# Loading the stacks of a transformer block's queries and keys in halves of 8 heads, into 48, 32 and 16 partitions at a time

## The chip, the cores and the metric

The kernel runs on one core of a Trainium2 chip. The metric is the device time of one execution in microseconds; lower is better.

## The reference

One block of a conditioned transformer over a batch of 8 sequences of 512 tokens with 256 features, in 16 heads of 16, all in float32:

```python
c6 = silu(c) @ Wc + bc                                    # shift, scale, gate, twice
xm = ln(x) * (1 + sc_msa) + sh_msa
q = (xm @ Wq + bq).reshape(B, S, 16, 16) / 16             # k, v likewise, not divided
w = softmax(einsum('bqhc,bkhc->bhqk', q, k))
y = einsum('bhqk,bkhc->bqhc', w, v).reshape(B, S, 256)
x = x + g_msa * (y @ Wo + bo)
xm2 = ln(x) * (1 + sc_mlp) + sh_mlp
x = x + g_mlp * (gelu(xm2 @ W1 + b1) @ W2 + b2)           # W1: 256 x 1024
```

## The kernel before

All work is done for one batch element after another in a software pipeline written out by hand. Pass i does four things side by side: it projects batch i+2 to queries, keys and values (`has_a`), computes the plain scores of batch i+1 and takes their row maxima (`scores`, `row_max`, 64 blocks of 128 x 512), computes the transposed scores, the exponentials and the product with the values of batch i, and the MLP of batch i-1. Passes run from -2 to 8; passes 2 to 5 are a loop of two bodies, the others are written out. A pass with all parts first goes through 16 attention steps, then the projections, then the MLP, and ends with the projection of the attention's output (`wo_products`), in whose middle `first_transposed` computes the first transposed scores of the next pass. Each engine has its own program, and semaphores tie them.

**Stacks.** The scores need float32 accuracy, and run in bf16. So each query and each key is split in three bf16 parts (high, middle, low), and the six products of parts that count are summed by one matmul over 96 partitions: six slots of 16 partitions, each the 16 features of a head, in `qst` the parts `QPARTS`, in `kst` the parts `KPARTS`. The free axis holds 16 heads x 512 tokens. The projections leave features on partitions (`j` = 0, 1 for the two halves of the queries, 2, 3 of the keys), so that the heads have to be moved: ScalarE, VectorE and GpSimd form the three parts of a j in `parts` (semaphores `part_h`, `part_m`, `part_l`), `write_parts` on SyncE writes them to DRAM (384 KB for each j), and `load_stack` reads them back, one DMA for each slot, six for the queries and six for the keys of a batch. `parts_written[w]` counts the writes of the queries and of the keys, `stack_loaded` all twelve loads. There are two pairs of stacks, used in turn.

**Maxima.** When the 64 maxima of a batch are there, TensorE turns them (`turn_maxima`), VectorE splits them in two bf16 rows (`maxima_rows`, `mrow_done`), and SyncE loads them into two more partitions of `qst`, opposite rows of -1 in `kst` (`load_maxima`, `m_loaded`; for the first half of batch 0's heads `half_loaded`). So the transposed scores come out with the maximum taken off. `first_transposed` waits for it.

**Order on SyncE's queue in a pass.** Outputs of the attention (`y_scr`), writes of j = 0 and 1, reciprocal sums to `r_scr` (after `rec_done`), writes of j = 2 and 3, `rb` (the reciprocals, broadcast, which VectorE needs for `y_norm(0)`), loads of the query stack, loads of the key stack, maxima, output of the batch before, next input. All DMAs are issued by SyncE. In the prologue, batch 1's parts are written only when batch 0's stacks are loaded, and its stacks are loaded only when GpSimd has read the weights staged in them (`const_set`, 6).

Of the kernel before, what the change touches and what calls it, by code (L numbers as in the profile page):

```python
# [25 lines left out]
ALU = mybir.AluOpType  # L26
# [3 lines left out]
NB, S, H = 8, 512, 256  # L30
# [3 lines left out]
KC = H // P  # L34
TT = S // P
JT = MLP // P
QPARTS = (0, 0, 1, 1, 0, 2)
KPARTS = (0, 1, 0, 1, 2, 0)
NSLOT = len(QPARTS)
MROW = NSLOT * DH  # L40
KROWS = MROW + 2
G = 4
# [23 lines left out]
def dit_block(nc, x, c, Wc, bc, Wq, bq, Wk, bk, Wv, bv, Wo, bo, W1, b1, W2, b2, out,  # L66
              c6_scr, parts_scr, y_scr, r_scr):
    with ExitStack() as ctx:
# [85 lines left out]
        rest_done = sem("rest_done")  # L154
        part_m = sem("part_m")
        part_l = sem("part_l")
        parts_written = [sem(f"parts_written_{n}") for n in "qk"]
        stack_loaded = sem("stack_loaded")
        v_done = sem("v_done")
        vaug_done = sem("vaug_done")  # L160
        s_done = sem("s_done")
# [87 lines left out]
        def _(sp):  # L249
# [24 lines left out]
            def step(i, par):  # L274
                if runs(i, 2) and later(i, 2, 1) and not early(i) or early(i) and not later(i, 2, 1):
                    b = i + 3 if early(i) else i + 2
                    sp.wait_ge(tp_done[0], b)
                    sp.dma_start(xa[:], x[bass.ds(b, 1)].rearrange("o (t p) f -> p (o t) f", p=P)).then_inc(xa_loaded, 16)
                if runs(i, 0):
                    if later(i, 0, 1):  # L280
                        sp.wait_ge(x1_done, i)
                    sp.dma_start(xd[:], x[bass.ds(i, 1)].rearrange("o (t p) f -> p (o t) f", p=P)).then_inc(xd_loaded, 16)
                    sp.dma_start(ga[:], c6_scr[bass.ds(i, 1), G1 * H:(G1 + 1) * H].broadcast_to([P, H])).then_inc(ga_loaded, 16)
                if runs(i, -1):
                    if later(i, -1, 1):
                        sp.wait_ge(o_gated, i - 1)
                    sp.dma_start(gm[:], c6_scr[bass.ds(i - 1, 1), G2 * H:(G2 + 1) * H].broadcast_to([P, H])).then_inc(gm_loaded, 16)

                def load_maxima(stack, first, last, loaded):

                    for n in range(2):
                        sp.dma_start(stack[MROW + n:MROW + n + 1, first:last, :], mrow[0:last - first, n, :]).then_inc(loaded, 16)

                if runs(i, 0) and not later(i, 0, 1):
                    sp.wait_ge(mrow_done, 2)
                    load_maxima(qst[par], NH // 2, NH, m_loaded)
                if runs(i, 0):


                    for g in range(NG):  # L300
                        sp.wait_ge(y_evac, NG * i + g + 1)
                        sp.dma_start(y_scr[G * g:G * (g + 1)].rearrange("h r s -> (h r) s"), ysb[:, g % 2, :]).then_inc(y_written[g % 2], 16)
                    for n in range(2):
                        sp.wait_ge(y_written[n], 32 * i + 32)
                    sp.dma_start(den, y_scr[:, DH, :].rearrange("h (a s) -> h a s", s=NH * S // P)).then_inc(den_loaded, 16)
                    sp.wait_ge(xg_done, i + 1)
                    for k in range(KC):
                        sp.dma_start(yc[:, k, :], y_scr[8 * k:8 * k + 8, 0:DH, :]).then_inc(yc_loaded, 16)

                def write_parts(b, j):  # L310
                    sp.wait_ge(part_l, 4 * b + j + 1)
                    m = j % 2
                    sp.dma_start(parts_scr[j // 2, :, m * P:(m + 1) * P, :].rearrange("n p s -> p n s"),
                                 parts[:, j, :, :]).then_inc(parts_written[j // 2], 16)

                def load_stack(b, w):


                    sp.wait_ge(parts_written[w], 32 * b + 32)
                    for slot in range(NSLOT):  # L320
                        stk, which = (qst, QPARTS) if w == 0 else (kst, KPARTS)
                        sp.dma_start(stk[par][slot * DH:(slot + 1) * DH, :, :],  # L322
                                     parts_scr[w, which[slot]].rearrange("(h d) s -> d h s", d=DH)).then_inc(stack_loaded, 16)

                if early(i) and later(i, 2, 1):
                    sp.wait_ge(stack_loaded, 192)
                if runs(i, 2):
                    write_parts(i + 2, 0)
                    write_parts(i + 2, 1)
                if runs(i, 0):  # L330
                    sp.wait_ge(rec_done, i + 1)
                    sp.dma_start(r_scr.rearrange("h (a s) -> (h a) s", s=NH * S // P), rec).then_inc(r_written, 16)
                if runs(i, 2):
                    write_parts(i + 2, 2)
                    write_parts(i + 2, 3)
                if runs(i, 0):
                    sp.wait_ge(r_written, 16 * i + 16)
                    for k in range(KC):
                        sp.dma_start(rb[:, k, :], r_scr[8 * k:8 * k + 8].unsqueeze(1).broadcast_to([8, DH, S])).then_inc(rb_loaded, 16)
                if runs(i, 2):  # L340
                    if early(i) and later(i, 2, 1):

                        sp.wait_ge(c6_written, 16)
                        sp.wait_ge(prep_pe, 4)
                        sp.wait_ge(w_split, 2)
                    load_stack(i + 2, 0)
                    if early(i) and later(i, 2, 1):
                        sp.wait_ge(const_set, 6)
                    load_stack(i + 2, 1)
                if early(i) and runs(i, 1):  # L350
                    sp.wait_ge(half_rows, 2)
                    load_maxima(qst[1 - par], 0, NH // 2, half_loaded)
                elif runs(i, 1):
                    sp.wait_ge(mrow_done, 2 * i + 4)
                    load_maxima(qst[1 - par], 0, NH, m_loaded)
                if runs(i, -1):
                    sp.wait_ge(o_done, i)
                    sp.dma_start(out[bass.ds(i - 1, 1)].rearrange("o (t p) f -> p (o t) f", p=P), osb[:]).then_inc(out_written, 16)
# [5 lines left out]
        def _(pool):  # L364
# [31 lines left out]
            def step(i, par):  # L396
# [32 lines left out]
                if runs(i, 2):  # L429
                    b = i + 2  # L430
                    for j in range(4):
                        if j == 2 and runs(i, -1):
                            z_lo(1, i - 1)
                        pool.wait_ge(part_m, 4 * b + j + 1)
                        pool.tensor_tensor(parts[:, j, 2, :], rest[:, j % 2, :], parts[:, j, 1, :], ALU.subtract).then_inc(part_l, 1)  # L435
                    if early(i) and later(i, 2, 1):
                        mlp_weights()
                if runs(i, -1):
# [12 lines left out]
        def _(act):  # L451
# [33 lines left out]

            def step(i, par):
                if runs(i, 0):
                    for w in range(2):
                        act.wait_ge(parts_written[w], 32 * (i + 2) if runs(i, 1) else 32 * NB)
                    for s in range(STEPS):  # L490
                        for p in range(2):
                            act.wait_ge(st_done, 32 * i + 2 * s + p + 1)
# [16 lines left out]
                if runs(i, 2):  # L509
                    b = i + 2  # L510
                    for j in range(4):
                        act.wait_ge(qk_done, 4 * b + j + 1)
                        if j % 2 == 0 and later(i, 2, 1) and not runs(i, 0):
                            act.wait_ge(parts_written[j // 2], 32 * b)
                        act.activation(parts[:, j, 0, :], ps[:, QK_BANKS[j], :], ACT.Identity,
                                       bias=bqk[:, j // 2, j % 2:j % 2 + 1]).then_inc(part_h, 1)
                    for n in range(2):
                        act.wait_ge(v_done, 2 * b + n + 1)
                        act.activation(vaug[par][:, 2 * n:2 * n + 2, :, 0:DH],
                                       ps[:, 4 + n, :].rearrange("p (t h d) -> p t h d", t=2, d=DH), ACT.Copy).then_inc(vaug_done, 1)  # L520
# [24 lines left out]
        def _(pe):  # L545
# [36 lines left out]
            def scores(i, par, blocks, banks=(6, 7)):  # L582

                for _ in range(blocks if runs(i, 1) else 0):
# [2 lines left out]
                    h, t = n // TT, n % TT  # L587
                    if n >= len(banks):
                        pe.wait_ge(max_done, 64 * (i + 1) + n - len(banks) + 1)
                    elif n == 0:  # L590
                        pe.wait_ge(stack_loaded, 192 * (i + 2))
                        if later(i, 1, 1):
                            pe.wait_ge(mrow_done, 2 * (i + 1))
                    pe.matmul(ps[:, banks[n % len(banks)], :], qst[1 - par][0:MROW, h, t * P:(t + 1) * P], kst[1 - par][0:MROW, h, :],  # L594
# [211 lines left out]
        def _(dve):  # L806
# [115 lines left out]
            def step(i, par):  # L922
# [36 lines left out]
                def rest_of(b, j):  # L959
# [4 lines left out]
                    elif early(i) and later(i, 2, 1):  # L964
                        dve.wait_ge(part_l, 4 * b + j - 1)
                    dve.scalar_tensor_tensor(out=rest[:, j % 2, :], in0=ps[:, QK_BANKS[j], :], scalar=bqk[:, j // 2, j % 2:j % 2 + 1],
                                             in1=parts[:, j, 0, :], op0=ALU.add, op1=ALU.subtract).then_inc(rest_done, 1)
                    dve.wait_ge(rest_done, 4 * b + j + 1)
                    dve.tensor_copy(parts[:, j, 1, :], rest[:, j % 2, :]).then_inc(part_m, 1)  # L969

# [98 lines left out]
_INS = ["x", "cond_1024"] + ["L0_cond_" + n for n in ("Wc", "bc", "Wq", "bq", "Wk", "bk", "Wv", "bv", "Wo", "bo", "W1", "b1", "W2", "b2")]  # L1069


# [21 lines left out]
```

## Time and profile before

| | us |
|---|---|
| median of 3 runs | 865.38 |
| lowest, highest | 861.15, 870.09 |
| profiled execution, first to last instruction (its own time is not given beside it) | 857.3 |
| TensorE, VectorE, ScalarE, GpSimd busy in it | 725.0, 582.5, 384.3, 222.2 |
| TensorE's mean granted clock | 0.906 |
| moved by DMA | 75.87 MB in 68,774 packets |

The profile is of one execution. Times in its rows are microseconds from the first instruction. In a timeline, a row gives the start, the length, the engine (SPq is SyncE's queue of DMA issues, whose length is that of issuing and not of moving), the line, the operation, what it writes and reads, how many are merged, and in brackets the idle time before it with what ended it. Neighbouring matmuls overlap, so merged lengths are rough. L594 are the plain scores, L624 the transposed ones, L732 and L724 the output projection, L895 the row maxima, L313 the writes of parts, L322 the loads of the stacks, L292 the loads of the maxima.

### The profile page before, as it was taken

How to read it: one execution, taken by the hardware profiler on the slowest of the kernel's cores; microseconds unless marked ns; L12 is line 12 of the kernel's file. 1: busy time of each engine (PE TensorE's matmuls, PEld its weight loads, DVE VectorE, ACT ScalarE, POOL GpSimd, SP SyncE). 2: the span in 40 equal slices, each digit the busy share in tenths (PEclk: the TensorE clock that was granted, in tenths of full speed). 3: DMA queues.
4: the chain of work that ended last, by engine and by line, in shares of the span. 5: the costliest groups of instructions: out<-in, count | busy, mean ns of one | idle time of the engine just before them, and what ended most of it. 6: DMA issues, size and time to landing. Idle time of an engine off the chain costs nothing.

```text
span 857.3 us, 11761 instructions
## 1 busy us (share of the span) xinstructions
PE 725.0 (85%) x3967; PEld 390.6 (46%) x3967; DVE 582.5 (68%) x1015; ACT 384.3 (45%) x462; POOL 222.2 (26%) x163
## 2 busy tenths in 40 slices
PE   4648589865999599995999599997999798999987
PEld 1531122422247432682257522682258422851776
DVE  5728588863987488874987388875987587560373
ACT  0410156303763177423763167424762376269321
POOL 4262001200316103430315103430325030331244
PEclk9775599956999899997999799998999899899998
DMA  7499700295018910395028910393028611111210
GB/s 262 121 122 161 117 14 26 95 160 94 25 52 152 143 53 25 125 136 113 26 70 143 138 52 25 129 145 100 26 88 148 107 45 36 43 63 37 65 31 24
DMA packets 68774, 75.87 MB, mean 88 GB/s; under 512 B 6214, under 2 KB 59996, under 8 KB 68716
## 3 DMA queue, kind: packets, MB, share of 16 engines
q1 hardware_dynamic: 68716, 75.10, 43.5%
q8 instruction: 35, 0.57, 0.3%
q14 instruction: 23, 0.19, 0.1%
HBM read 49.35 MB, written 25.48 MB: 87 GB/s over the span
## 4 chain that ended last, share of the span: by engine, by line
issue 36%; PE 30%; DVE 11%; POOL 10%; DMA 7%; SPq 3%; ACT 2%; POOLq 0%; DVEq 0%; ACTq 0%
PE ps L616 6%; PE ps L594 6%; PE ps L624 5%; DVE mx L895 5%; PE ps L549 4%; POOL hl L442 4%; PE ps L755 3%; DMA qst<-mrow 3%; SPq L322 3%; DMA kst<-parts_scratch 2%; POOL prob L435 2%; PE ps L759 2%; ACT prob L497 1%; POOL x L415 1%; POOL xd L428 1%
## 5 line engine op out<-in xcount | busy, mean ns | idle before, releaser
L895 DVE TENSOR_REDUCE mx<-ps 128x1 f32<-128x512 f32 x512 | 335.9, 686 | 83.8 <-PE ps L594 80.0
L497 ACT ACTIVATE prob<-ps 128x1024 f32<-128x1024 f32 x256 | 247.9, 1022 | 237.4 <-PE ps L624 237.0
L594 PE MATMUL ps<-kst,qst 96*128 96x512 bf16 x512 | 201.5, 417 | 33.9 <-DVE mx L895 17.5
L624 PE MATMUL ps<-qst,kst 98*128 98x512 bf16 x512 | 156.9, 402 | 60.6 <-DMA qst<-mrow 52.9
L594 PEld LDWEIGHTS ps<-kst,qst 96*128 96x128 bf16 x512 | 46.1, 99 | 204.0 <-DVE mx L895 166.7
L616 PE MATMUL ps<-prob,vaug 128*32 128x512 f32 x1024 | 137.3, 608 | 0.4 <-ACT prob L497 0.3
L442 POOL TENSOR_TENSOR hl<-z,hh 128x512 fp32r<-128x512 f32 x64 | 82.3, 1286 | 138.6 <-DVE hh L1024 138.6
L624 PEld LDWEIGHTS ps<-qst,kst 98*128 98x128 bf16 x512 | 48.8, 102 | 130.1 <-DMA qst<-mrow 54.2
L536 ACT ACTIVATE z<-ps,bias_t 128x512 f32<-128x512 f32 x64 | 44.0, 688 | 135.7 <-PE ps L759 130.1
L390 POOL TENSOR_TENSOR rstd<-vare,mhalf 128x4 f32<-128x4 f32 x16 | 16.3, 1021 | 330.4 <-DVE vare L835 330.4
L549 PE MATMUL ps<-w_hi,hh 128*128 128x256 f32 x256 | 73.6, 287 | 0.3 <-POOL hl L442 0.3
L435 POOL TENSOR_TENSOR prob<-prob 128x512 bf16<-128x512 f32 x32 | 37.3, 1167 | 140.3 <-DVE prob L969 140.3
L549 PE MATMUL ps<-w_hi,hl 128*128 128x256 f32 x256 | 72.0, 281 | 0.0
L549 PE MATMUL ps<-w_lo,hh 128*128 128x256 f32 x256 | 71.9, 281 | 0.0
L755 PE MATMUL ps<-zh,w_hi 128*128 128x512 f32 x128 | 61.1, 478 | 2.0 <-DVE zh L900 2.0
L1024 DVE CAST hh<-z 128x512 fp32r<-128x512 f32 x64 | 37.0, 579 | 35.3 <-ACT z L536 35.3
L1010 DVE TENSOR_TENSOR x<-ps,ga 128x1024 f32<-128x1024 f32 x7 | 8.6, 1225 | 75.3 <-PE ps L732 75.3
L755 PE MATMUL ps<-zh,w_lo 128*128 128x512 f32 x128 | 51.9, 405 | 0.0
L549 PEld LDWEIGHTS ps<-w_hi,hh 128*128 128x128 f32 x256 | 48.2, 188 | 2.9 <-POOL hl L442 0.8
L549 PEld LDWEIGHTS ps<-w_lo,hh 128*128 128x128 f32 x256 | 48.2, 188 | 1.8
L549 PEld LDWEIGHTS ps<-w_hi,hl 128*128 128x128 f32 x256 | 48.2, 188 | 0.0
L759 PE MATMUL ps<-zl,w_hi 128*128 128x512 f32 x128 | 41.7, 407 | 0.1
(106 smaller groups left out, 858.6 us busy)
## 6 DMA issues: line engine op xcount, KB each, us to landing
parts_scratch<-prob SPq DMA_DIRECT2D x32, 384.0 KB, 2.6
qst<-parts_scratch SPq DMA_DIRECT2D x48, 256.0 KB, 11.2
kst<-parts_scratch SPq DMA_DIRECT2D x48, 256.0 KB, 17.6
y_scratch<-rb SPq DMA_DIRECT2D x32, 256.0 KB, 2.0
xa<-in_x_dram SPq DMA_DIRECT2D x8, 512.0 KB, 9.4
xd<-in_x_dram SPq DMA_DIRECT2D x8, 512.0 KB, 3.5
yc<-y_scratch SPq DMA_DIRECT2D x16, 256.0 KB
rb<-r_scratch SPq DMA_DIRECT2D x16, 256.0 KB
```

What stands on the lines that cost most here:

```text
L435: pool.tensor_tensor(parts[:, j, 2, :], rest[:, j % 2, :], parts[:, j, 1, :], ALU.subtract).then_inc(part_l, 1)
L442: pool.tensor_tensor(hl[:, j % HR, :], hb[:, j % HB, :], hh[:, j % HR, :].bitcast(F32), ALU.subtract).then_inc(hl_done, 1)
L497: act.activation(prob[:, s % 2, 2 * p:2 * p + 2, :], ps[:, 2 * p:2 * p + 2, :], ACT.Exp, scale=1.0 / DH).then_inc(exp_done, 1)
L536: act.activation(hb[:, j % HB, :], ps[:, 4 + j % 2, :], ACT.Gelu, bias=b1_t[:, j:j + 1]).then_inc(gelu_done, 1)
L549: m = pe.matmul(out_, a, b, start=start and n == 0, stop=stop and n == 2, skip_group_check=True)
L594: pe.matmul(ps[:, banks[n % len(banks)], :], qst[1 - par][0:MROW, h, t * P:(t + 1) * P], kst[1 - par][0:MROW, h, :], start=True, stop=True ...
L616: m = pe.matmul(ps[32 * q:32 * q + 32, 4 + g % 2, :], vaug[par][:, kt, G * g + q, :], prob[:, s % 2, q, :], start=kt == 0, stop=kt == TT - ...
L624: m = pe.matmul(ps[:, q, :], kst[par][0:KROWS, G * g + q, kt * P:(kt + 1) * P], qst[par][0:KROWS, G * g + q, :], start=True, stop=True)
L755: pe.matmul(ps[:, 4 + j % 2, :], w1[n][:, k, f], zh_of(1, b)[:, k, :], start=k == 0 and n == 0, stop=False)
L759: m = pe.matmul(ps[:, 4 + j % 2, :], w1[0][:, k, f], zl_of(1, b)[:, k, :], start=False, stop=k == KC - 1)
L895: dve.tensor_reduce(mx[:, t, h:h + 1], ps[:, banks[n % len(banks)], :], AXX, ALU.max).then_inc(max_done, 1)
L1024: dve.tensor_copy(hh[:, j % HR, :], hb[:, j % HB, :]).then_inc(hh_done, 1)
```

## The change

- Within each j, the features are ordered by their place in the head first and by the head second, through permuted columns of Wq, bq, Wk and bk, laid out where the arrays are handed to the kernel. `parts_scr` becomes `(4, 3, 128, 512)`, one block for each j, in which the 8 heads of one feature lie together.
- The parts are stored in such an order (`PART_AT`) that slots 0 to 2 hold parts 0 to 2, slots 3 and 4 two neighbouring parts, slot 5 one. So three DMAs load a half: into 48, 32 and 16 partitions, 8 heads each (`SLOT_RUNS`).
- `load_stack(b, w, m)` loads half m of the queries (w = 0) or keys. Each j has its own semaphore of writes, each half of the heads its own of loads, and the scores of heads 0 to 7 wait for the first halves alone.
- On SyncE's queue each query half is issued ahead of the write of a keys' part; `rb` comes between those writes and the loads of the keys' halves. The prologue's waits move along.
- ScalarE waits for the four writes one by one.

```diff
-QPARTS = (0, 0, 1, 1, 0, 2)
-KPARTS = (0, 1, 0, 1, 2, 0)
-NSLOT = len(QPARTS)
+NSLOT = 6
+PART_AT = ((0, 1, 2), (2, 1, 0))
+SLOT_RUNS = (((0, 0, 3), (3, 0, 2), (5, 0, 1)), ((0, 0, 3), (3, 1, 2), (5, 2, 1)))
...
                 def write_parts(b, j):
                     sp.wait_ge(part_l, 4 * b + j + 1)
-                    m = j % 2
-                    sp.dma_start(parts_scr[j // 2, :, m * P:(m + 1) * P, :].rearrange("n p s -> p n s"),
-                                 parts[:, j, :, :]).then_inc(parts_written[j // 2], 16)
-
-                def load_stack(b, w):
-
-
-                    sp.wait_ge(parts_written[w], 32 * b + 32)
-                    for slot in range(NSLOT):
-                        stk, which = (qst, QPARTS) if w == 0 else (kst, KPARTS)
-                        sp.dma_start(stk[par][slot * DH:(slot + 1) * DH, :, :],
-                                     parts_scr[w, which[slot]].rearrange("(h d) s -> d h s", d=DH)).then_inc(stack_loaded, 16)
+                    sp.dma_start(parts_scr[j].rearrange("n p s -> p n s"), parts[:, j, :, :]).then_inc(parts_written[j], 16)
+
+                def load_stack(b, w, m):
+
+                    stk = (qst, kst)[w][par]
+                    sp.wait_ge(parts_written[2 * w + m], 16 * b + 16)
+                    for slot, part, n in SLOT_RUNS[w]:
+                        sp.dma_start(stk[slot * DH:(slot + n) * DH, 8 * m:8 * m + 8, :],
+                                     parts_scr[2 * w + m, part:part + n].rearrange("n (d h) s -> (n d) h s", d=DH))\
+                            .then_inc(stack_loaded[m], 16)
 
                 if early(i) and later(i, 2, 1):
-                    sp.wait_ge(stack_loaded, 192)
+                    for m in range(KC):
+                        sp.wait_ge(stack_loaded[m], 96)
...
                 if runs(i, 2):
+                    if early(i) and later(i, 2, 1):
+
+                        sp.wait_ge(c6_written, 16)
+                        sp.wait_ge(prep_pe, 4)
+                        sp.wait_ge(w_split, 2)
+                    load_stack(i + 2, 0, 0)
                     write_parts(i + 2, 2)
+                    load_stack(i + 2, 0, 1)
                     write_parts(i + 2, 3)
...
                 if runs(i, 2):
                     if early(i) and later(i, 2, 1):
-
-                        sp.wait_ge(c6_written, 16)
-                        sp.wait_ge(prep_pe, 4)
-                        sp.wait_ge(w_split, 2)
-                    load_stack(i + 2, 0)
-                    if early(i) and later(i, 2, 1):
                         sp.wait_ge(const_set, 6)
-                    load_stack(i + 2, 1)
+                    load_stack(i + 2, 1, 0)
+                    load_stack(i + 2, 1, 1)
...
-                    elif n == 0:
-                        pe.wait_ge(stack_loaded, 192 * (i + 2))
+                    if t == 0 and h % 8 == 0:
+                        pe.wait_ge(stack_loaded[h // 8], 96 * (i + 2))
+                    if n == 0:
...
+QK_FEATURES = tuple("L0_cond_" + n for n in ("Wq", "bq", "Wk", "bk"))
...
+        if name in QK_FEATURES:
+            a = a.reshape(a.shape[:-1] + (KC, NH // KC, DH)).swapaxes(-1, -2).reshape(a.shape)
...
-    args.append(nc.dram_tensor("parts_scratch", (2, 3, H, S), _mybir.dt.bfloat16).ap())
+    args.append(nc.dram_tensor("parts_scratch", (2 * KC, 3, P, S), _mybir.dt.bfloat16).ap())
```

## Rows read from the trace of the kernel before

**Rows 1.** The page: busy shares, and the DMA line of the 40 slices.

```profile
PE 725.0 (85%) x3967; PEld 390.6 (46%) x3967; DVE 582.5 (68%) x1015; ACT 384.3 (45%) x462; POOL 222.2 (26%) x163
...
DMA  7499700295018910395028910393028611111210
```

**Rows 2.** The list of waits: who waited for whom; us in total, times, longest us.

```profile
PE ps L624 <- DMA qst<-mrow: 52.9, 6, 12.5
...
PE ps L594 <- DMA kst<-parts_scratch: 13.7, 1, 13.7
```

**Rows 3.** Timeline of TensorE around the loads of the maxima: start us, us, line, tiles, idle.

```profile
202.62 1.89 PE L624 MATMUL ps<-qst,kst 98*128 98x512 bf16 x4 [12.50 <-DMA qst<-mrow]
...
490.01 1.89 PE L624 MATMUL ps<-qst,kst 98*128 98x512 bf16 x4 [9.07 <-DMA qst<-mrow]
...
758.55 1.04 PE L624 MATMUL ps<-qst,kst 98*128 98x512 bf16 x4
```

**Rows 4.** Timeline of SyncE's queue of DMA issues in three passes: start us, us, how many.

```profile
168.74 0.33 SPq L332 DMA_DIRECT2D r_scratch<-rb  x1
...
454.82 0.33 SPq L332 DMA_DIRECT2D r_scratch<-rb  x1
...
456.30 1.22 SPq L339 DMA_DIRECT2D rb<-r_scratch  x2
...
460.69 10.69 SPq L322 DMA_DIRECT2D kst<-parts_scratch  x6
477.66 1.20 SPq L292 DMA_DIRECT2D qst<-mrow  x2
...
755.42 1.20 SPq L292 DMA_DIRECT2D qst<-mrow  x2
```

**Rows 5.** Windows: length and each engine's busy us, TensorE's granted clock, DMA share, GB/s.

```profile
72.00:98.00 26.00, 18.18 (x34) 3.41 (x33) 20.68 (x35) 0.00 (x0) 0.00 (x0) 0.50 1.13 121
...
484.00:490.00 6.00, 0.00 (x0) 0.00 (x0) 0.00 (x0) 0.00 (x0) 0.00 (x0) 0.53 1.03 181
68.00:72.00 4.00, 4.00 (x9) 0.68 (x7) 4.00 (x8) 0.00 (x0) 2.23 (x1) 0.50 1.09 380
3.00:8.00 5.00, 0.00 (x0) 0.00 (x0) 3.60 (x1) 1.36 (x2) 5.00 (x1) 1.00 1.01 381
```

**Rows 6.** Timelines of the prologue: SyncE's queue, TensorE, GpSimd, ScalarE.

```profile
32.91 5.15 SPq L313 DMA_DIRECT2D parts_scratch<-prob  x4
...
88.96 1.47 SPq L292 DMA_DIRECT2D qst<-mrow  x2
...
66.56 19.34 PE L594 MATMUL ps<-kst,qst 96*128 96x512 bf16 x34 [13.65 <-DMA kst<-parts_scratch]
...
98.84 1.44 PE L624 MATMUL ps<-qst,kst 98*128 98x512 bf16 x3 [6.65 <-issue]
...
58.76 4.49 POOL L382 TENSOR_TENSOR w_lo<-kst,w_hi 128x2048 fp32r<-128x2048 f32 x1
...
49.65 1.26 ACT L515 ACTIVATE prob<-ps,bias_t 128x512 bf16<-128x512 f32 x2 [1.88 <-PE ps L701]
```

**Rows 7.** The page's DMA issues: how many, KB each, median us from issue to landing.

```profile
parts_scratch<-prob SPq DMA_DIRECT2D x32, 384.0 KB, 2.6
...
kst<-parts_scratch SPq DMA_DIRECT2D x48, 256.0 KB, 17.6
...
vaug<-in_L_cond_Wc_dram SPq DMA_DIRECT2D x1, 768.0 KB, 4.4
```

**Rows 8.** Timeline of VectorE in two passes.

```profile
470.71 1.22 DVE L990 TENSOR_TENSOR yc<-yc,rb 128x1024 f32<-128x1024 f32 x1
...
479.08 1.22 DVE L1048 TENSOR_TENSOR xn<-ps,gm 128x1024 f32<-128x1024 f32 x1
...
493.64 1.23 DVE L1010 TENSOR_TENSOR x<-ps,ga 128x1024 f32<-128x1024 f32 x1 [12.08 <-PE ps L732]
...
760.57 1.23 DVE L1010 TENSOR_TENSOR x<-ps,ga 128x1024 f32<-128x1024 f32 x1 [1.24 <-PE ps L732]
```

More of the change, by code:

```diff
@@ L156, in dit_block @@
         part_l = sem("part_l")
-        parts_written = [sem(f"parts_written_{n}") for n in "qk"]
-        stack_loaded = sem("stack_loaded")
+        parts_written = [sem(f"parts_written_{w}{m}") for w in "qk" for m in range(KC)]
+        stack_loaded = [sem(f"stack_loaded{m}") for m in range(KC)]
         v_done = sem("v_done")
@@ L434, in step @@
                         pool.wait_ge(part_m, 4 * b + j + 1)
-                        pool.tensor_tensor(parts[:, j, 2, :], rest[:, j % 2, :], parts[:, j, 1, :], ALU.subtract).then_inc(part_l, 1)
+                        pool.tensor_tensor(parts[:, j, PART_AT[j // 2][2], :], rest[:, j % 2, :], parts[:, j, 1, :], ALU.subtract).then_inc(part_l, 1)
                     if early(i) and later(i, 2, 1):
@@ L487, in step @@
                 if runs(i, 0):
-                    for w in range(2):
-                        act.wait_ge(parts_written[w], 32 * (i + 2) if runs(i, 1) else 32 * NB)
+                    for j in range(4):
+                        act.wait_ge(parts_written[j], 16 * (i + 2) if runs(i, 1) else 16 * NB)
                     for s in range(STEPS):
@@ L512, in step @@
                         act.wait_ge(qk_done, 4 * b + j + 1)
-                        if j % 2 == 0 and later(i, 2, 1) and not runs(i, 0):
-                            act.wait_ge(parts_written[j // 2], 32 * b)
-                        act.activation(parts[:, j, 0, :], ps[:, QK_BANKS[j], :], ACT.Identity,
+                        if later(i, 2, 1) and not runs(i, 0):
+                            act.wait_ge(parts_written[j], 16 * b)
+                        act.activation(parts[:, j, PART_AT[j // 2][0], :], ps[:, QK_BANKS[j], :], ACT.Identity,
                                        bias=bqk[:, j // 2, j % 2:j % 2 + 1]).then_inc(part_h, 1)
@@ L966, in rest_of @@
                     dve.scalar_tensor_tensor(out=rest[:, j % 2, :], in0=ps[:, QK_BANKS[j], :], scalar=bqk[:, j // 2, j % 2:j % 2 + 1],
-                                             in1=parts[:, j, 0, :], op0=ALU.add, op1=ALU.subtract).then_inc(rest_done, 1)
+                                             in1=parts[:, j, PART_AT[j // 2][0], :], op0=ALU.add, op1=ALU.subtract).then_inc(rest_done, 1)
                     dve.wait_ge(rest_done, 4 * b + j + 1)
@@ L1080 @@
     for name in _INS:
-        a = _np.ascontiguousarray(inputs[name])
+        a = _np.asarray(inputs[name])
+        if name in QK_FEATURES:
+            a = a.reshape(a.shape[:-1] + (KC, NH // KC, DH)).swapaxes(-1, -2).reshape(a.shape)
+        a = _np.ascontiguousarray(a)
         arrays[f"in_{name}_dram"] = a
```

## The prediction

> **What bounds the kernel now.** I read the page first. No engine fills the span: TensorE is busy 85%, VectorE 68%, and the DMA digits rise to 8 and 9 once in every pass and fall to 0 or 1 between [rows 1]. Next the list of waits, since the question is what ends the idle time. TensorE waits 52.9 us in six pieces for `qst<-mrow`, the load of the two rows of maxima, and 13.7 us once for a key stack [rows 2]. The load of the maxima is only 2x16 KB, so it can't be slow by itself. The timeline of SyncE's queue shows why it is late: in the pass around 450 us it is issued at 477.66, 6 us after the last of twelve stack loads, and TensorE gets it at 490.01. In the pass from 750 us, which has no stack loads, it is issued at 755.42 and the same matmul starts at 758.55 with no idle time before it [rows 3, 4]. So it queues behind the stacks. In the time between, no engine computes at all [rows 5], hence these are microseconds of the kernel and not of one engine. The prologue has the same pattern twice: the first scores wait until 66.56 for batch 0's keys, and the first transposed scores start at 98.84, when batch 1's loads are through (the row names no releaser, but the window view has the DMA engines full to 98), though the half's maxima had been issued at 88.96 [rows 6].
>
> The cause is the rate of the stack loads. All twelve of a batch are 12 x 262,144 B = 3.15 MB. Alone (72 to 98 us) they move at 121 GB/s with the DMA engines full (share 1.13), that is 26 us a batch; the writes of the parts just before, in packets of 1 KB too but from 128 partitions, move at 380 GB/s, as do the weights at the start at 381 [rows 5]. A stack load reaches 16 partitions.
>
> The Trainium skill ("SBUF — State Buffer", Door 1: The DMA port swizzle) says why that can be: four partitions share a DMA port, 16 partitions reach 4 of 16 ports and about 109 GB/s. The 121 GB/s lie a little above that ceiling, so the row agrees in size and not to the digit.
>
> **The change, part by part.** (1) Shape. Each stack goes in two halves of 8 heads, each half in three loads of 48, 32 and 16 partitions: 393, 262 and 131 KB, 786 KB in all. Count of DMAs (12) and bytes stay. The 8 heads of a partition now lie together in DRAM, 8 KB in one run. No row shows a load of 48 or 32 partitions, so I bound it: no better than today, 121 GB/s, is 6.5 us for a half; the 380 GB/s of 128 partitions is 2.1 us. Between them, 3.1 times the rate over three doublings of the partitions is 1.46 for each doubling: 16, 32 and 48 partitions give 121, 177 and 220 GB/s, so 1.08 + 1.48 + 1.79 = 4.3 us a half, 17.2 us a batch against 26. I take 4.3, for it uses both rows. The long run counts for nothing in it: Wc comes in rows of 6 KB and the parts in 1 KB and both are fast [rows 5, 7].
>
> The same section of the Trainium skill speaks against the shape of 48: partitions 32 apart share a port, so 48 reach no more ports than 32, and the first load would be held by the doubly used ones. By its 27.2 GB/s for a port a half would take 2.4 + 1.2 + 1.2 = 4.8 us; the sum below would then be some 6 us smaller. It isn't used in the sum.
>
> (2) Order. Old: k writes, rb, then q and k loads. New: q half 0, k write 0, q half 1, k write 1, rb, k half 0, k half 1. A DMA starts moving 1.3 us after its issue and takes 0.3 us after its last byte: a parts write lands after 2.6 us [rows 7], of which 393 KB at 380 GB/s are 1.0. In the pass around 450 the r write is at 454.82 [rows 4], so the first q load is issued at 455.2 and its data run from 456.5. In order: q0 to 460.8, k write to 461.8, q1 to 466.1, k write to 467.2, rb (524 KB at 380) to 468.6, k0 to 472.9, k1 to 477.2, landed by 477.7. Three waits are new on SyncE's queue: q0 for its write (long landed), k0 for the k write (landed 462.2, before rb is even through) and k1 for the second (landed 467.5, k0 still moving). They cost nothing as long as the rings hold work; behind them stand only the maxima and the output. The maxima are ready at 477.66 as today and land within the 3.1 us of the undisturbed pass, at 480.8. TensorE comes to them at 480.9 (490.01 less the 9.07 of its wait) [rows 3, 4]. The wait is gone and almost nothing is behind it: the gated output that the same point asks for ends at 480.3 (the VectorE instruction before the last in rows 8).
>
> What the move of rb costs: its landing goes from about 460 (issued 456.3 to 457.5) to about 469.1. VectorE wants it at 470.71 [rows 8]. That cover is 1.6 us, and is gone if a half takes over 5.1 us; then VectorE, and the MLP with it, stalls by the rest.
>
> (3) Sum over the six passes. The waits are 52.9 in total, the first of 12.5 [rows 2, 3]. In the pass of 202.62 the r write is 21.4 us before TensorE is ready (168.74 to 190.1); the loads end at 168.74 + 0.4 + 1.3 + 17.2 + 3.5 + 0.5 = 191.6, which leaves 1.5. For the others the same sum ends before the maxima are issued. So 51.4. Then the clock: at 484 to 490 it is granted at 0.53, so in these passes TensorE comes out of the wait at its 1.2 GHz level. From the first of its matmuls to VectorE's gating took 493.64 - 490.01 = 3.63 us there and 760.57 - 758.55 = 2.02 in the pass without the wait [rows 3, 5, 8]: 1.6 us, six times, 9.6.
>
> (4) Prologue. Batch 0's first write is at 32.91, landed 35.5; q0's data from 36.8 to 41.1, k write 42.1, q1 46.4, k write 47.5, k0 51.8 and landed 52.3, k1 landed 56.6. Scores of heads 0 to 7 now need only the first halves, and TensorE ends batch 1's projections at 52.9 (66.56 less 13.65) [rows 6]: first score 53.0, 13.5 earlier; from there to the issue of the half's maxima are 22.4 us of scores and maxima (66.56 to 88.96) whose pace nothing changes, so that issue moves to 75.4. Batch 1's writes wait for both halves as they waited for the stack: 56.6, then 2.6 to landing, 1.3, and 17.2 + 2.1 + 0.5, which is 80.4; the half's maxima land behind that at 81.0 against 98.84: 17.8 us. Its k loads also wait for GpSimd's second weight subtraction, which ends at 63.3, before they are due [rows 6]. The scalar engine's waits for each single k write before it overwrites that part come true at 42.5 and 47.8, before it needs them at 49.6 [rows 6].
>
> The permuted columns of Wq, bq, Wk and bk are laid out before the launch, and the other positions of the parts change no shape: nothing. Together 51.4 + 9.6 + 17.8 = 79 us of the profiled 857.3, and I take the same off the median of 865.4, which stands 8 us above the profiled span: 786.
>
> **Rivals.** (a) A half is slow, 5.2 us (150 GB/s). For: 48 partitions in one load may be held by the busiest of what they share, and the halves wait on each other's writes. Batch 0's halves are then loaded at 60.2 and batch 1's at 87.6 (prologue gain 10.8), with a residue of 5.1 in the first pass and 0.6 in five, VectorE held 0.2 each: about 62 us, 803. (b) The partitions are not what limits; the rate stays 121 GB/s. For: the old reads step 16 KB in DRAM as well, and packets are small; a different cause could survive. Against: the same packets at 380 GB/s. Then rb lands at 473.5 and holds VectorE 2.8 us, the loads end at 486.5, TensorE goes on 3.3 us earlier than today in five passes, 2.2 in the first, 0.6 in the prologue: 19 us, 846. (c) The halves run faster than I interpolate, up to 2.1 us: the prologue is then held by the scores alone (53.0 + 22.4 + 3.1 = 78.5, a gain of 20.3), no residue: 83 us, 782. (d) The other side: three long runs on each DMA engine into few partitions are slower than today's. It decides when a half takes 7.3 us (108 GB/s): then 456.5 + 29.2 + 4.0 = 489.7, today's landing. At 9 us a pass would lose 6.8, six times, and the prologue 19: 925. Against it stand the 6 KB rows of Wc, 768 KB landed in 4.4 us [rows 7].
>
> **How the numbers follow.** (main) 0.55 with (c) 0.2 beside it, (a) 0.15, (b) 0.06, (d) 0.02, and 0.02 that something makes no change (a wait at the same place for another reason). Runs of this kernel lie 0.5% to either side of the median, so 1% is what can be told from no change. The range takes in (c) and (a), with the 4 us by which the median may stand to the profile otherwise: 774 to 815. Faster by over 1% holds all but (d) and the last: 0.95.
>
> **What would show it.** The waits for `qst<-mrow` fall from 52.9 to a few us, the longest in the first pass. The first scores start at 53 and the first transposed ones at 81. A window in a stack load shows about 180 GB/s. VectorE's yc multiply shows no wait for rb, except at the end, where rb was waited for before. If packets are as long as the runs, the stack loads drop from 24,576 packets to some 3,100 and SyncE's issues stop stalling (10.69 us for six key loads today). The prediction fails if a half takes over 5.1 us, where rb becomes late, or if the passes stay near 95 us though the wait is gone, which would mean that another engine's chain had run beside it; rows 5 say that none did.

## The result, and the profile after

The changed kernel takes 785.69 us (median of 4 runs, 784.75 to 789.83) against 866.65 us for the kernel before beside it (the three runs of its table and one more): a ratio of 0.909, 95% interval 0.904 to 0.914. The profiled execution spans 784.6 us, against 857.3.

The page's summary. The digits are the 40 slices, and PEclk is TensorE's granted clock in tenths. The DMA digits still rise once in a pass, to 6 to 9 and for a shorter time [rows 1], and the packets fell by 21,505, from 68,774 (the prediction had 24,576 less some 3,100):

```profile
PE 712.2 (91%) x3967; PEld 383.7 (49%) x3967; DVE 582.3 (74%) x1015; ACT 384.3 (49%) x462; POOL 222.4 (28%) x163
...
PEclk9775799859999999999999999999999998999999
DMA  8389100681029302751057302850066202021110
...
DMA packets 47269, 75.85 MB, mean 97 GB/s; under 512 B 6214, under 2 KB 35420, under 8 KB 44140
```

The engines do the same work, in less time; TensorE's mean granted clock is 0.945 instead of 0.906. The waits (us in total, times, longest) name what went and what came. `qst<-mrow` is gone from the head of the list; its one remaining wait on TensorE stands in the timeline below. In its place VectorE waits for `rb`, once in every pass with stack loads and once at the end, as before [rows 2]. The two waits at the head of the list were longer before (330.4 and 237.0 us) and are of engines that aren't the bottleneck:

```profile
POOL rstd L393 <- DVE vare L839: 250.5, 16, 45.2
ACT prob L500 <- PE ps L628: 165.7, 112, 28.2
...
DVE yc L994 <- DMA rb<-r_scratch: 20.3, 7, 4.6
```

TensorE's timeline: the first scores, the first transposed scores, and the pass of 202.62 before [rows 3, 6]:

```profile
52.80 1.56 PE L598 MATMUL ps<-kst,qst 96*128 96x512 bf16 x5 [0.18 <-DMA kst<-parts_scratch]
...
78.84 1.86 PE L628 MATMUL ps<-qst,kst 98*128 98x512 bf16 x4 [0.64 <-issue]
...
175.39 1.04 PE L628 MATMUL ps<-qst,kst 98*128 98x512 bf16 x4 [1.60 <-DMA qst<-mrow]
```

SyncE's queue in the pass of 454.82 before [rows 4], and VectorE there [rows 8]:

```profile
404.65 0.33 SPq L333 DMA_DIRECT2D r_scratch<-rb  x1
405.11 1.28 SPq L321 DMA_DIRECT2D qst<-parts_scratch  x3
406.50 0.38 SPq L314 DMA_DIRECT2D parts_scratch<-prob  x1
406.93 1.42 SPq L321 DMA_DIRECT2D qst<-parts_scratch  x3
408.46 0.38 SPq L314 DMA_DIRECT2D parts_scratch<-prob  x1
408.96 1.22 SPq L347 DMA_DIRECT2D rb<-r_scratch  x2
412.61 7.27 SPq L321 DMA_DIRECT2D kst<-parts_scratch  x6
428.17 1.20 SPq L294 DMA_DIRECT2D qst<-mrow  x2
```

```profile
422.89 1.23 DVE L994 TENSOR_TENSOR yc<-yc,rb 128x1024 f32<-128x1024 f32 x1 [2.27 <-DMA rb<-r_scratch]
...
433.69 1.23 DVE L1014 TENSOR_TENSOR x<-ps,ga 128x1024 f32<-128x1024 f32 x1 [1.24 <-PE ps L736]
```

The row of six key loads holds a wait: two groups of three, each issued in 1.2 us, with 4.8 us between them, in which SyncE waited for the second write of keys. The maxima, issued at 428.17, cost TensorE nothing; `yc` starts 18.2 us after the r write, against 15.9 before (470.71 - 454.82). From the gating `x<-ps,ga` of one pass to that of the next were 96.6, 95.3, 95.4, 94.4 and 92.8 us; now they are 84.8, 86.0, 85.5, 89.4 and 86.3.

### The profile page after: what moved, and what is told of

It is laid out like the page before. It is cut to its first block, busy times and chain, and to the rows that moved or that the text cites. A ratio compares the mean times of both kernels' runs of the same rounds, so it can differ in the third digit from the quotient of the medians.

```text
span 784.6 us, 11779 instructions
## 1 busy us (share of the span) xinstructions
PE 712.2 (91%) x3967; PEld 383.7 (49%) x3967; DVE 582.3 (74%) x1015; ACT 384.3 (49%) x462; POOL 222.4 (28%) x163
## 4 chain that ended last, share of the span: by engine, by line
issue 34%; PE 28%; DVE 14%; POOL 11%; DMA 8%; ACT 3%; SPq 2%; POOLq 0%; DVEq 0%; ACTq 0%
DVE mx L899 8%; PE ps L620 7%; PE ps L598 5%; PE ps L628 5%; POOL hl L445 4%; PE ps L552 3%; DMA rb<-r_scratch 3%; PE ps L759 2%; DMA qst<-mrow 2%; POOL prob L438 2%; ACT prob L500 2%; PE ps L763 1%; POOL x L418 1%; POOL xd L431 1%; DMA kst<-parts_scratch 1%
## 5 line engine op out<-in xcount | busy, mean ns | idle before, releaser
L598 PE MATMUL ps<-kst,qst 96*128 96x512 bf16 x512 | 197.4, 407 | 22.4 <-DVE mx L899 17.0
L628 PE MATMUL ps<-qst,kst 98*128 98x512 bf16 x512 | 150.4, 385 | 3.8 <-DMA qst<-mrow 1.6
L628 PEld LDWEIGHTS ps<-qst,kst 98*128 98x128 bf16 x512 | 46.8, 99 | 70.2 <-ACT prob L500 27.2
L620 PEld LDWEIGHTS ps<-prob,vaug 128*32 128x32 f32 x1024 | 20.4, 108 | 46.3 <-issue 42.3
```

The costliest lines, as they stand in the source:

```text
L620: m = pe.matmul(ps[32 * q:32 * q + 32, 4 + g % 2, :], vaug[par][:, kt, G * g + q, :], prob[:, s % 2, q, :], start=kt == 0, stop=kt == TT - ...
L628: m = pe.matmul(ps[:, q, :], kst[par][0:KROWS, G * g + q, kt * P:(kt + 1) * P], qst[par][0:KROWS, G * g + q, :], start=True, stop=True)
```

## The experiments

In each, everything else is as in the kernel named. Some edits are shown in short, with "..." or words in brackets for what is left out. A median stands with its lowest and highest run.

**1. All loads 16 partitions wide.** The changed kernel with

```diff
-SLOT_RUNS = (((0, 0, 3), (3, 0, 2), (5, 0, 1)), ((0, 0, 3), (3, 1, 2), (5, 2, 1)))
+SLOT_RUNS = (((0, 0, 1), (1, 1, 1), (2, 2, 1), (3, 0, 1), (4, 1, 1), (5, 0, 1)), ...)
```

> Each half of a stack in six loads of 16 partitions instead of 48, 32 and 16; the order, the halves and the 8 KB runs in DRAM stay. Width theory (the rate depends on how many partitions a load reaches): 121 GB/s again, 6.5 us a half, the maxima late by some 6 us in each pass and the first transposed scores back at about 98: 835 to 850 us. Run-length theory (the 8 KB runs made the loads fast): the changed kernel's 786, at most 792 for the twelve more issues.

Measured: 831.5 us (829.5 to 833.0). Run length alone is refuted; the wide loads are worth 46 us (the edit makes the loads narrower, and also smaller and twice as many). The maxima were not what was late, though: TensorE waited for them once, for 2.4 us, and VectorE waited for rb for 47.4 us in seven places:

```profile
DVE yc L995 <- DMA rb<-r_scratch: 47.4, 7, 8.4
...
PE ps L629 <- DMA qst<-mrow: 2.4, 1, 2.4
```

And a half took less than 6.5 us: from batch 0's first query load to both halves in place were 25.0 us (36.08 to 61.05 on SyncE's queue); less 1.6 for start and end and 2.1 for two writes that is 5.3 a half. The changed kernel needs 20.6 us for the same (35.19 to 55.76), 4.2 a half.

**2. 48, 32 and 16 partitions, in 1 KB runs.**

```diff
-    args.append(nc.dram_tensor("parts_scratch", (2 * KC, 3, P, S), ...
+    args.append(nc.dram_tensor("parts_scratch", (2 * KC, 3, P, 2 * S), ...    # read and written as [..., 0:S]
```

> The scratch of the parts has rows of 2 KB of which 1 KB is used, so that the loads into 48, 32 and 16 partitions read 1 KB runs as before the change. Width theory: within 3 us of 786. Run-length theory: back towards 846, stack windows at 121 GB/s. Packets of the kernel should return to some 68,700.

Measured: 788.8 us (785.8 to 793.9), a ratio of 0.915 (0.907 to 0.922), 68,774 packets, batch 0 in 20.8 us. The long runs bring nothing to the time that can be told here.

**3. rb ahead of the second query half.**

```diff
                     load_stack(i + 2, 0, 0)
                     write_parts(i + 2, 2)
+                (wait r_written, both loads of rb)
                     load_stack(i + 2, 0, 1)
                     write_parts(i + 2, 3)
-                (wait r_written, both loads of rb)
```

> The loads of rb issued ahead of the second query half and the second write of keys, nothing else. Theory: VectorE's waits for rb (20.3 us in seven places, 17.1 of them in the six passes with stack loads) lengthen the passes by 0.3 to 1.7 us each; they vanish and the time falls by 5 to 7 us to about 780, the first pass gaining nothing since its maxima then wait for the key halves. Rival: the pass was never held by rb, the same microseconds show as a wait for the maxima or for GpSimd, 786 within 1.

Measured: 783.3 us (781.6 to 785.7), 0.906 of the kernel before (0.901 to 0.912), an interval that holds the changed kernel's ratio. So the times don't tell the two kernels apart, and 5 to 7 us were expected where the medians differ by 2.4. The profile is sharper: no wait for rb but the last, while those for the maxima grew:

```profile
PE ps L629 <- DMA qst<-mrow: 5.2, 3, 4.4
...
DVE yc L995 <- DMA rb<-r_scratch: 3.4, 1, 3.4
```

The five passes from one gating to the next take 427.9 us together instead of 432.0, while in the first pass the maxima's wait grew from 1.6 to 4.4. That is the mechanism as expected, at half the size or less.

**4. Three loads of 32 partitions for each half.** The parts are stored as middle, high, low, for which the six products are two pairs of neighbouring parts and one more:

```diff
-PART_AT = ((0, 1, 2), (2, 1, 0))
-SLOT_RUNS = (((0, 0, 3), (3, 0, 2), (5, 0, 1)), ((0, 0, 3), (3, 1, 2), (5, 2, 1)))
+PART_AT = ((1, 0, 2), (1, 0, 2))
+SLOT_RUNS = (((0, 0, 2), (2, 0, 2), (4, 1, 2)), ((0, 0, 2), (2, 1, 2), (4, 0, 2)))
```

> Each half in three loads of 32 partitions (parts stored as middle, high, low; the six products stay the same). Sharing theory (a load lasts as long as the busiest of the groups of partitions that share a way in; 48 partitions put two thirds of their load on half of the ways): a half takes 3.3 to 3.6 us instead of 4.3 to 5, rb lands 2 us sooner, the first pass's maxima 3 us sooner: 776 to 781 us, and a first load of 262 KB lands 2.7 us after its issue. Interpolation theory (rate grows smoothly with partitions): 4.4 us a half, 786 within 2, first load lands after 3.1 us.

Measured: 782.7 us (779.6 to 784.3), a half 3.6 us by the same two points (35.13 to 53.34). The time lies between the theories, in the range of neither, and its ratio of 0.906 (0.901 to 0.911) isn't clear of the changed kernel's. The 3.6 us of a half are those of the sharing theory (3.3 to 3.6, against 4.4). A single load tells more. The first query load of a pass meets an empty ring, since only the small r write is before it. Its size and its us from issue to landing, by the DMA issues of a short window of the pass around 400 to 435, first in the changed kernel (48 partitions):

```profile
qst<-parts_scratch SPq DMA_DIRECT2D x1, 384.0 KB, 4.6
```

then with 32 partitions:

```profile
qst<-parts_scratch SPq DMA_DIRECT2D x1, 256.0 KB, 3.3
```

then with 16 (the first experiment):

```profile
qst<-parts_scratch SPq DMA_DIRECT2D x1, 128.0 KB, 2.9
```

Over all six passes they are 4.4 to 4.9, 3.1 to 3.3 and 2.9 to 3.2. Twice the bytes into twice the partitions cost some 0.3 us; half as many again, with partitions 32 to 47 added, cost 1.4. Less 1.6 for start and end that is 3.0, 1.6 and 1.4 us of moving: rates of 131, 164 and 94 GB/s, so the load of 48 is the slower of the two wide ones. The smooth curve that I had drawn from 16 to 128 partitions puts it at 220, which would land it after 3.4 us. At 32 partitions the curve holds: it had 3.1 us, and the sharing theory's 2.7 was too low. It is the load of 48 that refutes it.

The Trainium skill ("SBUF — State Buffer", Door 1: The DMA port swizzle) has partitions 32 apart on one port: 0 to 47 then put double load on half of eight ports, and the durations above agree with that, in that the load of 48 moves for 3.0 us and the load of 32 for 1.6.

**5. The changed kernel again**, as the one to compare 6 to 8 with.

> The changed kernel once more, as the one to compare with on the same chip: 785 to 787 us, all theories.

Measured: 786.4 us (782.9 to 790.9), 0.916 of the kernel before on that chip (0.911 to 0.920).

**6. Both improvements (3 and 4).**

> Three loads of 32 partitions for each half, and the loads of rb ahead of the second query half. If both act as seen alone (4 us in the passes from rb, 5 to 7 us from the shape, of which some 3 are the same waits for rb): 777 to 780 us, with no wait for rb but the last and the maxima late in the first pass by 2 us at most. If rb and shape remove the same wait and nothing else: the 782 to 783 us of either alone.

Measured: 780.8 us (778.6 to 783.3), 0.909 (0.905 to 0.913): 5.6 us under the changed kernel on the same chip, the lowest median here and just above the range of 777 to 780. Neither addition nor a single shared wait: in the first pass the maxima come 4.3 us late, and that took back part of it.

**7. New shapes, old order.**

```diff
-                    load_stack(i + 2, 0, 0)
                     write_parts(i + 2, 2)
-                    load_stack(i + 2, 0, 1)
                     write_parts(i + 2, 3)
...
                 (rb)
+                    load_stack(i + 2, 0, 0)
+                    load_stack(i + 2, 0, 1)
                     load_stack(i + 2, 1, 0)
                     load_stack(i + 2, 1, 1)
```

> The new shapes and halves in the order of the kernel before: both writes of keys' parts, rb, then the four halves. Theory that the shape brings the gain: rb lands early, the rings hold the same bytes and end at the same time, the prologue loses 1 us or 2: within 3 us of the changed kernel. Theory that the order matters (query halves hidden behind the k writes): the key halves end later by what the query halves had started earlier, 2 to 4 us a pass, 795 to 805 us.

Measured: 786.5 us (785.3 to 787.4), 0.915 (0.912 to 0.919), the same as the changed kernel. Two effects of the order can be read, one against the other. In the old order the first transposed scores start at 83.52 instead of 78.84, and the maxima are 4.0 us late in the first pass. The five passes take 428.4 us instead of 432.0 and 432.5 in the two profiles of the changed kernel, with no wait for rb but the last. In the old order batch 0's stack loads stand alone, so that a window shows their rate, 181 GB/s, which is 4.3 us a half:

```profile
42.00:54.00 12.00, 11.40 (x48) 9.46 (x48) 7.12 (x11) 4.00 (x7) 3.48 (x3) 0.72 1.02 181
```

**8. Loads of 16 partitions and 1 KB runs, new order.** Experiments 1 and 2 together.

> Loads of 16 partitions as in the first experiment, and 1 KB runs as well (rows of 2 KB in the scratch), so that only the halves and the order differ from the kernel before. The 16-partition loads with 8 KB runs came out at 5.3 us a half and 831 us, not at the 6.5 us and 846 us of the kernel before's rate. If the run length is what made that difference: 6.5 us a half, 840 to 850 us. If it is the smaller loads (131 KB each, so that the engines move on sooner to a load for other partitions): 5.3 us again, 828 to 834 us.

Measured: 832.0 us (831.5 to 835.4). The run length doesn't matter for the time at this width either (the first query load of a pass lands after 3.4 to 3.6 us, against 2.9 to 3.2 with runs of 8 KB). What sets 5.3 us a half apart from the 6.5 of the kernel before is the size of the loads, the order, or the place of the rows in DRAM: the 8 heads of a partition now stand 2 KB apart, where those of the kernel before stood 16 KB apart.

**9. The same in the old order.** The edit of experiment 7 on top of 8.

> As the last one (halves of 8 heads, each in six loads of 16 partitions and 131 KB, 1 KB runs), in the order of the kernel before. Against the kernel before only the size of a load (half) and the wait for the first halves differ. If loads of 131 KB really move at 5.3 us a half, where the 262 KB loads of the kernel before took 6.5: rb is no longer late, the stacks end near the moment that TensorE asks for the maxima, and the time is 800 to 812 us. If the 832 us came from the new order: 845 us or more.

Measured: 818.5 us (813.0 to 821.9), above the 800 to 812 of the first theory and far below the 845 of the other. So it isn't the order: with the same width, run length and order as the kernel before, in loads of 131 KB instead of 262, the kernel takes 46 us less. A window of it that holds stack loads alone moves 147 GB/s for batch 0, and one for batch 1 131, where the kernel before has 122 (the same window, 42 to 58) and 121 (72 to 98) [rows 5]:

```profile
42.00:58.00 16.00, 11.54 (x48) 9.50 (x48) 7.37 (x11) 4.40 (x7) 7.32 (x5) 0.79 1.12 147
...
72.00:84.00 12.00, 10.03 (x20) 1.97 (x19) 11.86 (x21) 0.00 (x0) 0.00 (x0) 0.50 1.13 131
```

Why the two batches differ is open. Three things at least changed together: the size of a load, the rows' place in DRAM, and that the scores of heads 0 to 7 wait for the first halves alone. No run takes them apart. Against the place in DRAM speaks the first query load in experiment 10, with the heads 16 KB apart: it lands its 262 KB after 4.1 to 4.5 us, which less 1.6 is 90 to 105 GB/s, about the 94 of a load of 131 KB above. So the size is argued, not shown.

```profile
PE ps L629 <- DMA qst<-mrow: 24.2, 6, 11.5
```

TensorE still waits 24.2 us for the maxima, 11.5 of them in the first pass, which I had put too low. With loads this slow the new order costs 13.5 us (832.0 against 818.5), for rb is then 5 to 9 us late in each pass.

**10. Order alone.** The kernel before with its six query loads ahead of the writes of keys' parts.

> The kernel before, with the six loads of the query stack moved ahead of the writes of the keys' parts; shapes, sizes, waits for whole stacks as before. Theory (the order alone brings next to nothing): rb lands 3 us late for VectorE, the stacks end at most 3 us sooner in a pass, 850 to 862 us. Rival (the order is a gain of its own): below 845 us.

Measured: 851.9 us (846.5 to 859.6), 0.986 (0.977 to 0.996). Some 13 us, the upper end of what I had allowed: the waits for the maxima fell from 52.9 to 11.4 us, and those for rb rose from 3.9 to 40.3. The first query load of a pass is the one to set beside those of experiment 4:

```profile
qst<-parts_scratch SPq DMA_DIRECT2D x1, 256.0 KB, 4.5
```

The same 262 KB that land after 3.1 to 3.3 us in 32 partitions take 4.1 to 4.5 in 16 (with 1 KB runs, which cost that load some 0.5 us in experiment 8).

**11 and 12. Who follows whom.** Experiment 9 with its six slots issued in another sequence; not a byte, width or size differs. In short:

```diff
-slots 0, 1, 2, 3, 4, 5     # neighbours never 32 partitions apart
+slots 0, 2, 1, 3, 4, 5     # experiment 11: 0 and 2, 1 and 3 are
+slots 0, 1, 4, 5, 2, 3     # experiment 12: those pairs four loads apart within a half
```

> The 16-partition kernel in the old order (818 us, 147 GB/s in the stack loads), its six loads of a half issued for the slots 0, 2, 1, 3, 4, 5, so that loads for partitions 0 to 15 and 32 to 47, and 16 to 31 and 48 to 63, follow each other. Sharing theory (those pairs share a way in, other neighbours don't, and the DMA engines that are ahead fill another group's way meanwhile): less overlap, 120 to 135 GB/s, 828 to 850 us. Rival (the rate of 16-partition loads doesn't depend on who follows): 818 within 4.

> The same kernel with the slots issued 0, 1, 4, 5, 2, 3, so that loads that share a way in are four apart instead of two. Sharing theory with engines running ahead by more than one load: faster than 818, 800 to 812 us, 155 GB/s or more; if they run ahead by one load only: 818 within 4. Rival: 818 within 4.

Measured: 841.1 us (840.3 to 842.6) and 814.8 us (806.8 to 815.6), against 818.5 on another chip; as ratios to the kernel before 0.972 (0.967 to 0.977) and 0.938 (0.931 to 0.945), against 0.943 (0.934 to 0.951). The windows of batch 0's and batch 1's loads, of 11 and then of 12:

```profile
42.00:58.00 16.00, 10.01 (x47) 8.34 (x45) 6.01 (x9) 3.84 (x6) 9.22 (x6) 0.82 1.11 134
...
72.00:84.00 12.00, 10.00 (x21) 2.06 (x20) 11.86 (x21) 0.00 (x0) 0.00 (x0) 0.50 1.13 126
```

```profile
42.00:58.00 16.00, 10.32 (x48) 8.43 (x47) 5.78 (x9) 3.84 (x6) 9.53 (x6) 0.82 1.10 148
...
72.00:84.00 12.00, 9.04 (x18) 1.82 (x18) 11.54 (x19) 0.00 (x0) 0.00 (x0) 0.50 1.12 135
```

Experiment 11 is slower by 23 us, at a rate 9% lower in batch 0 and 4% in batch 1. Its sequence also changes which part in DRAM neighbours read, but that doesn't explain it: neighbours of a half read the same part twice in 11, three times in 12 and once in 9, queries and keys together, and 12 isn't slower. So who follows whom in the partitions matters: consecutive loads overlap more when they go to partitions that aren't 32 apart.

Experiment 12 gives no more than the 4 us that I had called no effect, but it can't tell how far the overlap reaches. The halves are issued in a row, and its slots 2 and 3 stand just before slots 0 and 1 of the next half. The pairs are four apart within a half and two apart over the seam; in experiment 9 it is the other way round. Run on from half to half, the two sequences are the same but for their ends.

## Why the prediction was right, point by point

**What bounds.** Right. The 52.9 us of waits for the maxima are 1.6, where 1.5 were predicted, and the passes fell from some 95 us to some 86.

**The rate.** 4.3 us for a half was predicted, 4.2 measured in the prologue; the window of experiment 7 has 181 GB/s, where about 180 were predicted. The number was right by luck and its derivation wrong: a curve over the partitions of one load, where two things act, the sharing among partitions 32 apart and the overlap of neighbouring loads (experiments 4 and 11). Taken singly, loads of 48, 32 and 16 partitions move for 3.0, 1.6 and 1.4 us (experiment 4), which would be 6.0 us a half; the 4.2 come of their overlap. The curve would have called three loads of 32 no better than 48, 32 and 16 (4.4 us); they take 3.6.

**Start and end of a load.** 1.3 us from issue to the first byte and 0.3 after the last were put in the sum. Batch 0's first write, issued at 32.91, moves from about 33.8 to 34.9 and has landed after 2.5 us: some 0.9 and 0.6. The two together, 1.5 to 1.6, are what the sum used, so no time hangs on it.

**Prologue.** 17.8 us predicted, 20.0 measured (98.84 to 78.84). The first scores came at 52.80 (53.0 predicted), the half's maxima were issued at 74.97 (75.4). Batch 1 didn't hold them: TensorE stood for 0.64 us before the first transposed scores, so the gain is nearly the 20.3 of the case in which the scores alone set it. Batch 1's first load was issued at 58.35, 0.9 us sooner than in the sum, and from 60 to 76 us its writes and loads move 223 GB/s, where the sum has 3.93 MB in 19.3 us, 204 GB/s.

**Clock.** 1.6 us a pass was right where the wait is gone: the clock digits above are 9, once 8, from the tenth slice on. In the first pass, which keeps a short wait, it is open. From the first transposed matmul to the gating are 2.03 us in the profile above (177.42 - 175.39, after a wait of 1.60), as in the undisturbed pass, but 3.64 in the changed kernel's second profile (179.21 - 175.57, after a wait of 1.22), where the window from 175 to 179 has a granted clock of 0.50.

**rb.** This step of the prediction failed: the path of rb through the ring, and the 1.6 us of cover that it left. I had it land at 469.1 on the old scale, 1.6 us early; it was 1.7 to 4.6 us late in every pass with loads, 17.1 us together. Set against the old distance from r write to gating, less wait and clock, the passes lost 3.9, 0.3, 1.3, 0.9, 1.6 and 1.7 us, 9.7 in all; experiment 3 gives back 4.1 of the last five's 5.8. In the first pass TensorE itself shows it: its wait for `zh`, which VectorE makes from the `yc` that needed rb, grew by 4.7 us, and rb was 4.6 late. Here it is before the change and then after it; in experiment 3 it is 3.7 again.

```profile
PE ps L724 <- DVE zh L995: 3.7, 1, 3.7
```

```profile
PE ps L728 <- DVE zh L999: 8.4, 1, 8.4
```

The sum had every load of the ring go through in full before the next starts. The window from the first query load to rb's landing shows that it isn't so:

```profile
405.00:423.00 18.00, 18.00 (x108) 15.01 (x108) 10.74 (x19) 4.15 (x7) 8.13 (x7) 1.00 1.00 214
```

18 us at 214 GB/s are 3.85 MB, and all that stands before rb's end is 2.88 MB (two query halves, two writes, rb). The other 1 MB is of the keys' halves behind it: they were moving before rb had landed. So some DMA engines must have gone on ahead, and rb lands with the last. That the lag comes from the load of 48, whose partitions are unequally shared, fits experiment 4, where the waits for rb fell from 20.3 to 11.5 us, but of the 8.9 us by which they fell in the six passes, two halves that take 0.6 us less each would bring 7.2 in any case. I have no view of the engines one by one, so it is argued and not shown.

**The sum.** Predicted 51.4 + 9.6 + 17.8 = 79 us off the profiled 857.3. Measured 72.7: 51.3 for the waits, 9.6, 20.0, less 9.7 for rb, and 1.5 that I can't place. The medians moved by 81, because the profiled execution of before was a fast one (9 us under its median, while that of after is 1 us under). On the chip of experiments 5 to 8 the medians moved by 75 (861.75 to 786.42). The 786 that came out is therefore right to a microsecond by luck; the sum behind it was 6 us too large.

**Rivals.** (b), the rate stays at 121, is refuted by the result, and half of its premise holds: experiment 9 shows that the width isn't the only thing, since halves loaded at the same width are faster. Of (c), only the outcome in the prologue came true, the scores alone setting it; the halves weren't faster than 4.2 us. (a)'s mechanism, the load of 48 held by its busiest partitions, is there, at a smaller price. (d) didn't occur.

**What the change is made of.** Some 46 us lie between the kernel before (864 in the chip's runs of the first four experiments, 865 beside experiment 9) and the halves of the same width (818.5, experiment 9), and some 32 between that and 48, 32 and 16 partitions (786.5, experiment 7, with runs of 8 KB besides, which change no time in experiments 2 and 8). Which of the three things that experiment 9 changes brings the first 46 is not taken apart. The order, which was half of the change, adds nothing to that (785.7 and 786.4): it starts the prologue 4.7 us sooner and pays as much for rb.

## What to carry to other kernels

A small transfer that waits behind large ones on the same rings shows up as a wait of its own name; look for when it was issued, and at a pass where the large ones are absent. Before a load into few partitions is widened, ask which partitions share a way in: here 32 partitions in a row from partition 0 moved in 1.6 us, hardly more than the 1.4 of 16, and 48 took 3.0. Three loads of 32 need no other change in the kernel than the order of the parts. Where narrow loads can't be avoided, issue neighbours for partitions that aren't 32 apart; cutting them small probably helps as well. And what is moved down in a queue needs a margin beyond the bytes ahead of it: rb landed 1.7 to 4.6 us after it was wanted, where the bytes gave it 1.6 us to spare.

## What the runs showed of the hardware that I had not expected

- A load of 393 KB into 48 partitions landed later (4.4 to 4.9 us) than its bytes or its width explain; one of 262 KB into 32 landed in 3.1 to 3.3, one of 131 KB into 16 in 2.9 to 3.2.
- Loads of 16 partitions moved at 121 to 122 GB/s in pieces of 262 KB, at 147 (batch 0) and 131 (batch 1) in pieces of 131 KB, and at 134 and 126 in these when neighbours went to partitions 32 apart. A single one moves at 90 to 105, so neighbours overlap.
- Three query loads of 48, 32 and 16 partitions take 1.28 us to issue on SyncE with 8 KB runs and 1.92 with 1 KB (experiment 2); six key loads of 1 KB packets behind a full ring took 10.69. The time of the kernel doesn't show it.
